# Two query projections moved in between the value tables by grid columns

## The chip, the cores and the metric

The kernel runs on one core of one Trainium2 chip, as one launch. Its time is the device time of that core in microseconds (us). Three runs of the kernel before gave 1713.64, 1715.28 and 1719.45 us; the median, 1715.28 us, is what the changed kernel is held against.

The engines are called as in the profile: PE is TensorE with its matmuls (PEld its weight loads), ACT is ScalarE, DVE is VectorE, POOL is GpSimd, SP is SyncE, which here only issues DMAs.

## The reference, cut to what matters

The model is a small audio tower of five steps on 4 batches of 750 tokens with 192 features. The change lies in the fourth, an attention with 12 heads of 64 features whose positions enter by two small tables, one by grid row and one by grid column (a grid of 27 columns):

```python
q = (x @ wq).reshape(B, N, H, HD).transpose(0, 2, 1, 3)
k = (x @ wk).reshape(B, N, H, HD).transpose(0, 2, 1, 3)
v = (x @ wv).reshape(B, N, H, HD).transpose(0, 2, 1, 3)
attn = jnp.einsum('bhid,bhjd->bhij', q, k) * scale
attn = attn + jnp.einsum('bhid,ijd->bhij', q, rel_pos_embed(N, rk_v, rk_h)) * scale
attn = jax.nn.softmax(attn, axis=-1)
out = jnp.einsum('bhij,bhjd->bhid', attn, v)
out = out + jnp.einsum('bhij,ijd->bhid', attn, rel_pos_embed(N, rv_v, rv_h))
out = out.transpose(0, 2, 1, 3).reshape(B, N, H * HD) @ wproj + bproj
```

## The kernel before, in words

The attention runs over 4 batches, each in two halves of 6 heads: eight half turns. A half turn has a long part, `words` (36 words of 125 keys each: scores, exponentials, values), and a passage from one half to the next. The first three batches are one hardware loop, the last batch is written out. There are seven passages that have a new half to prepare: four from half 0 to half 1 of one batch, three from half 1 to half 0 of the next batch. An eighth ends the attention and has no new half.

Every engine runs its own list of instructions in the order in which the code writes it, and the lists are tied by counting semaphores: `wait("name", k)` holds an engine until the k-th event of that name in this batch. Nothing is rearranged by a planner.

Keys and queries of a half are projected in six parts each (`keys_part`, `queries_part`; part n is pair n // 2 of heads, token half n % 2). A part is one `project` call: 5 matmuls of a full 128 x 128 weight tile over 376 columns (L2049) into bank n % 2 of the PSUM tile `a_M`. For keys, ACT copies the result to `khi` (L2391, two instructions) and DVE makes the rest `klo` (L2649, two). For queries, ACT copies to `pairs` (L2399, one). Before PE may write a bank again, its last reader must be done. Eight parts (half 0) or five parts (half 1) already run inside `words` between the last words (`fill`); what is left runs in the passage.

The passage of PE, in the order of its list before:

- the query parts that are left: parts 4 and 5 on the way from half 0 to 1, parts 1 to 5 on the way from half 1 to 0; then key parts 4 and 5;
- `value_tables` of the old half. One small product (L2104, L2107), then six sets by grid rows (`V_SETS`, L2117, weights of 96 rows x 64 columns), then six sets by grid columns (`H_SETS`, L2129, weights of 32 rows x 64 columns). ACT copies the first six out (L2432), DVE adds the last six to them (L2683). The fourth set by rows (m = 3) reuses the PSUM bank of the small product, and so waits for `rel_h_added` 1, which is DVE's copy of that product (L2677);
- `query_tables` of the new half (L2154, 128 rows x 64 columns, first by rows, `a_rqv`, then by columns, `a_rqh`), which wait for all six query parts in `pairs`; ACT and DVE copy them out in parallel (L2444, L2746);
- `boundary`: the values of the new half (L2193), the output projection of the old half (L2209) and the first row scores (L2167).

ACT's list in the passage: its output copies of the last word, the copies of the same parts, the six V copies, then `boundary`: six copies `work_rows` of the queries (L2405) and the table rows.

DVE's list in the passage from half 0 to half 1 reads: output of the last word (L2800, L2801), `keys_part` 4, `inverse`, `keys_part` 5, `value_tables`. `inverse` is a reciprocal (L2671) of softmax sums that come back by DMA: SP writes the sums to memory after the outputs (L1924, L1926), then fetches them as `dcol` (L1889). In the passage from half 1 to half 0 the order is: outputs, a bias add (L2641), `inverse`, `keys_part` 4 and 5, `value_tables`.

Of the kernel before, what the change touches and what calls it, by code (L numbers as in the profile page):

```python
# [1773 lines left out]
def window_attention(nc, keep, A, h, ident, W4, room, share, Y0, s_back, mv1, rstd1, w11, X1):  # L1774

    ctx = ExitStack()
    with ctx:
# [65 lines left out]
        def waiter(eng, i):  # L1843
            def wait(name, k):
                eng.wait_ge(sg[name], i * PER[name] + k)
            return wait
# [185 lines left out]
        def _(pe):  # L2032
# [17 lines left out]
                                            hn[:, m, lo:lo + HALF2], start=(x == 0), stop=(x == len(TERMS) - 1))  # L2050
                last.then_inc(sg[done], 1)

            def keys_part(i, half, n):

                wait = waiter(pe, i)
                if n == 0:
                    pe.wait_ge(s_wkv, 64 * i + 32 * half + 16)
                    wait("columns_ready", 3)
                elif n == 4 or n == 5:
                    wait("pairs_ready", half * 6 + n + 1)  # L2060
                elif n >= 2:
                    wait("khi_ready", half * 6 + n - 1)
                    wait("klo_ready", half * 6 + n - 1)
                project(wkv, n // 2, n % 2, 0, "k_product")

            def queries_part(i, half, n):

                wait = waiter(pe, i)
                if n == 0:
                    pe.wait_ge(s_wq, 32 * i + 16 * (half + 1))  # L2070
                if n < 2:
                    wait("khi_ready", half * 6 + n + 3)
                    wait("klo_ready", half * 6 + n + 3)
                else:
                    wait("pairs_ready", half * 6 + n - 1)
                project(wq, n // 2, n % 2, 1, "q_product")
# [17 lines left out]
                    elif x >= 35:  # L2094
                        queries_part(i + 1, 0, x - 35)

            def value_tables(i, half):

                wait = waiter(pe, i)
                wait("exp_ready", half * 36 + 36)  # L2100
                wait("out_dve", half * HG + HG)
                wait("out_act", half * HG + HG)
                for par in range(2):
                    nc.tensor.matmul(r_banks[0][64 * par:64 * par + 64, 0:NPR], rv[0:RH, 0, :],  # L2104
                                     work[0:RH, par::2, L - 1], start=True, stop=False)
                for par in range(2):
                    last = nc.tensor.matmul(r_banks[0][64 * par:64 * par + 64, 0:NPR], rv[RH:128, 0, :],  # L2107
                                            work[RH:128, par::2, CLS], start=False, stop=True)
                last.then_inc(sg["rel_product"], 1)
                for m, (gs, n) in enumerate(V_SETS):  # L2110
                    if m == 3:
                        wait("rel_h_added", half * (NHS + 1) + 1)
                    if m > 3:
                        wait("rel_v_copied", half * NV + m - 3)
                    for a, g in enumerate(gs):
                        for par in range(2):
                            last = nc.tensor.matmul(  # L2117
                                r_banks[(1 + m) % 4][64 * par:64 * par + 64, a * NPR * n:(a + 1) * NPR * n],
                                rv[0:RH, g + 1, :], group_tokens(work[0:RH, par::2, :], "v", g, n),
                                start=True, stop=True)  # L2120
                    last.then_inc(sg["rel_product"], 1)
                for m, (gs, n) in enumerate(H_SETS):
                    if m < 4:
                        wait("rel_v_copied", half * NV + NV + m - 3)
                    else:
                        wait("rel_h_added", half * (NHS + 1) + m - 2)
                    for a, g in enumerate(gs):
                        for par in range(2):
                            last = nc.tensor.matmul(  # L2129
                                r_banks[(1 + NV + m) % 4][64 * par:64 * par + 64, a * NPR * n:(a + 1) * NPR * n],  # L2130
                                rv[RH:128, g + 1, :], group_tokens(work[RH:128, par::2, :], "h", g, n),
                                start=True, stop=True)
                    last.then_inc(sg["rel_product"], 1)

            def query_tables(i, half):

# [183 lines left out]
            def turn(i, last_batch):  # L2320

                words(i, 0, last_batch)
                queries_part(i, 1, 4)
                queries_part(i, 1, 5)
                keys_part(i, 1, 4)
                keys_part(i, 1, 5)
                value_tables(i, 0)
                query_tables(i, 1)
                boundary((i, 0), (i, 1))
                words(i, 1, last_batch)  # L2330
                if last_batch:
                    value_tables(i, 1)
                    boundary((i, 1), None)
                else:
                    queries_part(i + 1, 0, 1)
                    queries_part(i + 1, 0, 2)
                    queries_part(i + 1, 0, 3)
                    queries_part(i + 1, 0, 4)
                    queries_part(i + 1, 0, 5)
                    keys_part(i + 1, 0, 4)  # L2340
                    keys_part(i + 1, 0, 5)
                    value_tables(i, 1)
                    query_tables(i + 1, 0)
                    boundary((i, 1), (i + 1, 0))

# [16 lines left out]
            with pe.Fori(0, B - 1) as i:  # L2362
                turn(i, False)
# [3 lines left out]
        def _(act):  # L2367
# [27 lines left out]
            def queries_part(i, half, n):  # L2395

                waiter(act, i)("q_product", half * 6 + n + 1)
                pr, a = n // 2, n % 2
                nc.scalar.activation(pairs[:, pr, a * HALF:(a + 1) * HALF], psM[:, a, a:a + HALF], ACT.Copy  # L2399
                                     ).then_inc(sg["pairs_ready"], 1)  # L2400

            def work_rows(i, half, x):

                waiter(act, i)("pairs_ready", half * 6 + 2 * (x // 2) + 2)
                nc.scalar.activation(work[0:64, x, 0:L], pairs[64 * (x % 2):64 * (x % 2) + 64, x // 2, :], ACT.Copy  # L2405
                                     ).then_inc(sg["work_ready"], 1)
# [30 lines left out]
            def boundary(old, new):  # L2437

                i, half = new
                wait = waiter(act, i)  # L2440
                if old is not None:
                    for x in range(HG):
                        work_rows(i, half, x)
                relative_rows(act, wait, half, 0, lambda o, x: nc.scalar.activation(o, x, ACT.Copy),  # L2444
                              "table_rows_act")
                wait("table_rows_act", (half + 1) * NTS)
                wait("table_rows_dve", (half + 1) * NTS)
                wait("work_ready", half * HG + HG)
                if old is not None:
                    waiter(act, old[0])("out_divided", old[1] * NPR + NPR)  # L2450
                else:

                    act.wait_ge(s_sum3, 3)
                for x in range(HG):
                    nc.scalar.activation(qhi[0:ONE, x, :], work[0:ONE, x, 0:L], ACT.Copy
                                         ).then_inc(sg["qhi_ready"], 1)
                    wait("v_product", half * CH + x + 1)
                    nc.scalar.activation(vhi[:, x, :, 0:64],
                                         psS[1][0:P, x % 2, 0:HG * HD].rearrange("p (h d) -> p h d", d=HD),
                                         ACT.Copy).then_inc(sg["vhi_ready"], 1)  # L2460
                    if old is None and x in (1, 2, 3):
                        for hh in (2 * x - 2, 2 * x - 1):
                            last = nc.scalar.activation(vhi[:, :, hh, 64:128], ohT, ACT.Copy)
                        if x == 3:
                            last.then_inc(s_og, 1)
                    if old is None and x == 4:
                        act.wait_ge(s_ln, 2)
                        nc.scalar.activation(rstd[:, CH:NT], rstd[:, CH:NT], ACT.Sqrt).then_inc(s_sd, 1)
# [58 lines left out]
            def turn(i, last_batch):  # L2527

                words(i, 0, last_batch)
                queries_part(i, 1, 4)  # L2530
                queries_part(i, 1, 5)
                keys_part(i, 1, 4)
                keys_part(i, 1, 5)
                value_tables(i, 0)
# [14 lines left out]
                else:  # L2549
                    queries_part(i + 1, 0, 1)  # L2550
                    queries_part(i + 1, 0, 2)
                    queries_part(i + 1, 0, 3)
                    queries_part(i + 1, 0, 4)
                    queries_part(i + 1, 0, 5)
                    keys_part(i + 1, 0, 4)
                    keys_part(i + 1, 0, 5)
                    value_tables(i, 1)
# [414 lines left out]
```

## Time and profile before

| | |
|---|---|
| median of 3 runs | 1715.28 us |
| the profiled execution | 1716.88 us, of which the span of the instructions is 1715.1 us |
| PE busy | 1539.9 us, 90% |
| DVE busy | 1172.9 us, 68% |
| ACT busy | 988.2 us, 58% |
| POOL busy | 374.2 us, 22% |
| mean granted clock of TensorE | 0.946 of full speed |

The attention fills the time from about 380 to 1490 us of the span. In it PE is busy nearly throughout. The granted clock is given as a share of full speed: 1.0 is 2.4 GHz, 0.5 is 1.2 GHz, and a value between them is the mean of a stretch that has both.

### The profile page before, as it was taken

The page shows a single profiled execution, that of the slowest core. Times are in us where ns is not written, and L with a number is a line of the kernel's source. Part 1 is how long each engine was busy: PE and PEld are TensorE (multiplying, and loading weights), DVE is VectorE, ACT ScalarE, POOL GpSimd, SP SyncE. Part 2 cuts the span into 40 slices and gives each one's busy share as a digit, 9 for nine tenths or more (in the row PEclk, how much of TensorE's full clock was granted, in tenths as well). Part 3 has the DMA queues.
Part 4 walks back from the last instruction along what each step waited for, and adds up shares of the span by engine and source line. Part 5 has one row for each costly group of instructions (what it writes and reads, how often), then busy time and mean ns, then how long its engine had stood idle before and what let it go on. Part 6 is the DMA issues. An engine that isn't in the chain of part 4 may idle for free. (4 is left out here: it accounts for less than half of the span.)

```text
span 1715.1 us, 32118 instructions
## 1 busy us (share of the span) xinstructions
PE 1539.9 (90%) x10815; PEld 1417.4 (83%) x10816; DVE 1172.9 (68%) x2224; ACT 988.2 (58%) x1777; POOL 374.2 (22%) x520
## 2 busy tenths in 40 slices
PE   5982999937999999999999999999999999848997
PEld 5862999936899898899998889988989988727996
DVE  4887555548775786786787677678677588585553
ACT  5541222225677578578677667767767857462231
POOL 5131566640001100110200110110100100013443
PEclk9995999977999999999999999999999999868998
DMA  9312111164101101100010110010010111091221
GB/s 267 70 55 77 48 57 57 57 142 121 44 11 38 45 11 39 46 11 19 25 49 11 31 45 20 30 44 20 29 45 11 39 49 37 21 295 49 61 58 28
DMA packets 61933, 94.81 MB, mean 55 GB/s; under 512 B 15644, under 2 KB 46511, under 8 KB 61422
## 3 DMA queue, kind: packets, MB, share of 16 engines
q1 hardware_dynamic: 52606, 72.92, 14.8%
q0 software_dynamic: 9200, 20.21, 4.1%
q8 instruction: 78, 1.28, 0.3%
q14 instruction: 49, 0.40, 0.1%
HBM read 72.58 MB, written 21.06 MB: 55 GB/s over the span
## 5 line engine op out<-in xcount | busy, mean ns | idle before, releaser
L2698 DVE TENSOR_REDUCE a_nmx<-a_M 125x1 f32<-125x752 f32 x256 | 240.8, 941 | 129.9 <-PE a_M L2167 129.2
L2517 ACT ACTIVATE a_Phi<-a_S 125x756 fp32r<-125x756 f32 x288 | 231.1, 803 | 156.9 <-PE a_O L2290 147.2
L2823 DVE TENSOR_TENSOR a_Plo<-a_PT,a_Phi 125x756 fp32r<-125x756 f32 x288 | 281.5, 977 | 52.5 <-ACT a_PT L2517 51.7
L2517 ACT ACTIVATE a_PT<-a_S 125x756 f32<-125x756 f32 x288 | 229.8, 798 | 0.0
L1970 POOL TENSOR_TENSOR a_qlo<-a_work,a_qhi 127x750 fp32r<-127x750 f32 x48 | 79.1, 1657 | 592.2 <-PE a_S L2271 507.9
L2271 PE MATMUL a_S<-a_qhi,a_khi 128*125 128x378 f32 x576 | 155.1, 350 | 13.6 <-issue 6.6
L2283 PE MATMUL a_O<-a_Phi,a_vhi 125*128 125x378 f32 x576 | 150.3, 342 | 1.3 <-ACT a_PT L2517 1.3
L2290 PE MATMUL a_O<-a_Plo,a_vhi 125*128 125x378 f32 x576 | 147.4, 337 | 1.0 <-DVE a_Plo L2823 0.9
L2271 PE MATMUL a_S<-a_qlo,a_khi 128*125 128x378 f32 x576 | 147.0, 336 | 0.0
L2271 PE MATMUL a_S<-a_qhi,a_klo 128*125 128x378 f32 x576 | 146.7, 336 | 0.0
L2286 PE MATMUL a_O<-a_Phi,a_vlo 125*64 125x378 f32 x576 | 146.4, 335 | 0.0
L2167 PE MATMUL a_M<-a_khi,a_qhi 127*125 127x376 f32 x512 | 132.2, 339 | 0.2 <-DVE a_nmx L2698 0.2
L1215 PE MATMUL m_psY<-m_w,m_hidT 128*128 x696 | 130.0, 330 | 2.6 <-DVE m_hidT L1572 2.6
L1215 PEld LDWEIGHTS m_psY<-m_w,m_hidT 128*128 128x128 f32 x696 | 114.4, 189 | 9.5 <-issue 9.5
L2271 PEld LDWEIGHTS a_S<-a_qhi,a_khi 128*125 128x125 f32 x576 | 98.3, 187 | 27.1 <-issue 13.6
L2290 PEld LDWEIGHTS a_O<-a_Plo,a_vhi 125*128 125x128 f32 x576 | 104.1, 189 | 14.5 <-DVE a_Plo L2823 4.3
L1299 ACT ACTIVATE m_xT<-m_psX 128x128 fp32r<-128x128 f32 x85 | 23.6, 278 | 156.4 <-PE m_psX L1139 156.4
L1979 POOL TENSOR_TENSOR a_outs<-a_outs,a_qhi 128x750 f32<-128x750 f32 x21 | 33.1, 1607 | 363.3 <-DVE a_outs L2683 363.3
L2283 PEld LDWEIGHTS a_O<-a_Phi,a_vhi 125*128 125x128 f32 x576 | 101.9, 190 | 11.1 <-issue 8.1
L1151 PE MATMUL m_psG<-m_w,m_xT 128*128 x540 | 110.4, 351 | 0.6 <-issue 0.4
L2271 PEld LDWEIGHTS a_S<-a_qhi,a_klo 128*125 128x125 f32 x576 | 103.9, 187 | 0.0
L2271 PEld LDWEIGHTS a_S<-a_qlo,a_khi 128*125 128x125 f32 x576 | 103.7, 187 | 0.0
(441 smaller groups left out, 3141.9 us busy)
## 6 DMA issues: line engine op xcount, KB each, us to landing
a_qhi<-a_rdens SPq DMA_DIRECT2D x48, 187.5 KB, 3.3
a_wkv<-a_w4k SPq DMA_DIRECT2D x8, 768.0 KB, 5.3
a_wq<-a_w4q SPq DMA_DIRECT2D x8, 768.0 KB, 6.7
a_wkv<-a_w4v SPq DMA_DIRECT2D x8, 768.0 KB, 5.8
m_w<-in_m_w SPq DMA_DIRECT2D x8, 576.0 KB, 9.2
m_X<-m_xn SPq DMA_DIRECT2D x8, 504.0 KB
m_w<-in_m_w SPq DMA_DIRECT2D x8, 384.0 KB, 7.3
m_w_ahead<-in_m_w SPq DMA_DIRECT2D x8, 384.0 KB, 8.0
```

The source lines that it names most:

```text
L1151: last = nc.tensor.matmul(psG[buf][:, g, 0:half], tokens, w1[0:rows_, bass.ds(e, 1), k, g * half:(g + 1) * half].rearrange("d o f -> d (o ...
L1215: last = nc.tensor.matmul(psY[:, 0:E], hidT[:, k * 128:(k + 1) * 128], w2[:, bass.ds(here, 1), k, :].rearrange("f o e -> f (o e)"), start= ...
L1970: pool.tensor_tensor(qlo[0:ONE, u % HG % QLO, :], work[0:ONE, u % HG, 0:L], qhi[0:ONE, u % HG, :].bitcast(F32), ALU.subtract).then_inc(sg[ ...
L1979: pool.tensor_tensor(outs[:, pr, 0:L], outs[:, pr, 0:L], rdb[:, pr, :], ALU.mult).then_inc(sg["out_divided"], 1)
L2167: last = nc.tensor.matmul(bank[0:P, a, 0:376], qhi[0:ONE, u % HG, c * P:(c + 1) * P], khi[0:ONE, u % HG, a * 374:a * 374 + 376], start=Tru ...
L2271: last = nc.tensor.matmul(psS[wd % 2][0:P, a, 0:HP], kk[:, u % HG, at], qq[:, PART[a]:PART[a] + HP], start=(x == 0), stop=(x == 2))
L2283: nc.tensor.matmul(psO[:, a, 0:HP], vhi[:, c, u % HG, :], Phi[:, wd % 2, at[a]], start=(c == 0), stop=False)
L2286: nc.tensor.matmul(psO[0:HD, a, 0:HP], vlo[:, c, u % HG, :], Phi[:, wd % 2, at[a]], start=False, stop=False)
L2290: last = nc.tensor.matmul(psO[:, a, 0:HP], vhi[:, c, u % HG, :], Plo[:, wd % 2, at[a]], start=False, stop=(c == CH - 1))
L2517: last = nc.scalar.activation(to[:, wd % 2, :].rearrange("p (a l) -> p a l", a=2), psS[wd % 2][0:P, :, 0:HP], ACT.Exp, scale=SCALE)
L2698: v.tensor_reduce(nmx[:, u % 2, c:c + 1], bank[0:P, :, 0:376], AX.XY, ALU.max, negate=True).then_inc(sg["max_ready"], 1)
L2823: v.tensor_tensor(Plo[:, wd % 2, :], PT[:, wd % 2, :], Phi[:, wd % 2, :].bitcast(F32), ALU.subtract).then_inc(sg["exp_rest"], 1)
```

## The change

On PE the two last query parts of every new half leave their place ahead of the key parts and go into `value_tables`, one behind the first set by grid columns (m = 0), one behind the third (m = 2). Key parts 4 and 5 move up. Since the order in which the banks of `a_M` are used is now keys 4, keys 5, queries 4, queries 5, the waits for a free bank are changed to match (`woven=True`): key parts 4 and 5 wait for query parts 2 and 3 to be copied, query parts 4 and 5 for key parts 4 and 5 to be split. ACT's copies of the two query parts move likewise, in between its `work_rows`. DVE, POOL and SP are not edited. The first half of the program, which has no old half, keeps its order, and so has the eighth passage.

```diff
-            def keys_part(i, half, n):
+            def keys_part(i, half, n, woven=False):
...
-                elif n == 4 or n == 5:
-                    wait("pairs_ready", half * 6 + n + 1)
+                elif n >= 4:
+                    wait("pairs_ready", half * 6 + (n - 1 if woven else n + 1))
...
-            def queries_part(i, half, n):
+            def queries_part(i, half, n, woven=False):
...
-                if n < 2:
-                    wait("khi_ready", half * 6 + n + 3)
-                    wait("klo_ready", half * 6 + n + 3)
+                if n < 2 or woven:
+                    wait("khi_ready", half * 6 + n + (1 if woven else 3))
+                    wait("klo_ready", half * 6 + n + (1 if woven else 3))
...
-            def value_tables(i, half):
+            def value_tables(i, half, new):
...
                     last.then_inc(sg["rel_product"], 1)
+                    if new is not None and m in (0, 2):
+                        queries_part(*new, 4 + m // 2, woven=True)
...
                 words(i, 0, last_batch)
-                queries_part(i, 1, 4)
-                queries_part(i, 1, 5)
-                keys_part(i, 1, 4)
-                keys_part(i, 1, 5)
-                value_tables(i, 0)
+                keys_part(i, 1, 4, woven=True)
+                keys_part(i, 1, 5, woven=True)
+                value_tables(i, 0, (i, 1))
...
                     queries_part(i + 1, 0, 3)
-                    queries_part(i + 1, 0, 4)
-                    queries_part(i + 1, 0, 5)
-                    keys_part(i + 1, 0, 4)
-                    keys_part(i + 1, 0, 5)
-                    value_tables(i, 1)
+                    keys_part(i + 1, 0, 4, woven=True)
+                    keys_part(i + 1, 0, 5, woven=True)
+                    value_tables(i, 1, (i + 1, 0))
...
                 if old is not None:
                     for x in range(HG):
+                        if x in (2, 4):
+                            queries_part(i, half, 3 + x // 2)
                         work_rows(i, half, x)
```

(The last piece is ACT's; two more pieces take `queries_part` 4 and 5 out of ACT's `turn`.)

PE's list in the passage from half 0 to half 1, from the last query part to the first query table. Before (`a_wq` are the query weights, `a_wkv` the key weights, `a_rv` the value tables; `x12` counts matmuls):

```order
646 L2049 MATMUL a_M<-a_hn,a_wq 128x376 x10
...
648 L2049 MATMUL a_M<-a_hn,a_wkv 128x376 x5
...
650 L2049 MATMUL a_M<-a_hn,a_wkv 128x376 x5
...
653 L2117 MATMUL a_O<-a_work,a_rv 64x81 x12
654 L2117 MATMUL a_S<-a_work,a_rv 64x81 x24
655 L1845 ISA
656 L2117 MATMUL a_O<-a_work,a_rv 64x81 x18
657 L2117 MATMUL a_S<-a_work,a_rv 64x60 x2
658 L2129 MATMUL a_S<-a_work,a_rv 64x84 x12
659 L2129 MATMUL a_O<-a_work,a_rv 64x84 x24
660 L2129 MATMUL a_S<-a_work,a_rv 64x84 x4
```

and now:

```order
646 L2049 MATMUL a_M<-a_hn,a_wkv 128x376 x10
...
649 L2117 MATMUL a_O<-a_work,a_rv 64x81 x12
650 L2117 MATMUL a_S<-a_work,a_rv 64x81 x24
651 L1845 ISA
652 L2117 MATMUL a_O<-a_work,a_rv 64x81 x18
653 L2117 MATMUL a_S<-a_work,a_rv 64x60 x2
654 L2129 MATMUL a_S<-a_work,a_rv 64x84 x12
...
656 L2049 MATMUL a_M<-a_hn,a_wq 128x376 x5
657 L2129 MATMUL a_O<-a_work,a_rv 64x84 x24
...
659 L2049 MATMUL a_M<-a_hn,a_wq 128x376 x5
660 L2129 MATMUL a_S<-a_work,a_rv 64x84 x4
```

The ten query matmuls have left the head of the passage and stand as two groups of five between the products by grid columns. The ISA row is the wait for `rel_h_added` 1 ahead of the fourth set by rows; it now stands ten matmuls nearer to the end of the words.

ACT's list from the last V copy on, before:

```order
342 L2432 ACTIVATE a_outs<-a_S 128x3x20
343 L2405 ACTIVATE a_work<-a_pairs 64x750 x6
344 L1845 ISA
345 L2444 ACTIVATE a_work<-a_S 29x3x162 x2
```

and now:

```order
341 L2430 ACTIVATE a_outs<-a_S 128x3x20
342 L2403 ACTIVATE a_work<-a_pairs 64x750 x2
343 L2397 ACTIVATE a_pairs<-a_M 128x375
344 L2403 ACTIVATE a_work<-a_pairs 64x750 x2
345 L2397 ACTIVATE a_pairs<-a_M 128x375
346 L2403 ACTIVATE a_work<-a_pairs 64x750 x2
```

The two copies of query parts stand behind the second and the fourth of the six row copies.

## Rows read from the trace of the kernel before

**Rows 1.** Seven passages, words' end to value products: us, PE busy, clock, DMA, GB/s.

```profile
530.97:552.90 21.93, 21.93 (x364) 0.84 0.18 56
666.94:690.21 23.27, 23.27 (x379) 0.93 0.21 53
804.67:827.17 22.50, 22.50 (x364) 0.85 0.19 55
940.36:963.89 23.53, 23.53 (x378) 0.93 0.20 53
1078.27:1097.70 19.43, 19.42 (x363) 1.00 0.21 64
1210.91:1234.43 23.52, 23.52 (x378) 0.93 0.18 53
1346.49:1367.45 20.96, 20.96 (x363) 0.92 0.21 59
```

**Rows 2.** PE in order of time, half 0 to 1, third batch: start, us.

```profile
1078.27 1.88 PE L2049 MATMUL a_M<-a_hn,a_wq 128*128 128x376 f32 x10
1080.08 1.99 PE L2049 MATMUL a_M<-a_hn,a_wkv 128*128 128x376 f32 x10
1082.01 0.28 PE L2104 MATMUL a_O<-a_work,a_rv 96*64 96x3 f32 x4
...
1083.32 1.85 PE L2117 MATMUL a_S<-a_work,a_rv 96*64 96x81 f32 x48
1085.00 1.43 PE L2117 MATMUL a_O<-a_work,a_rv 96*64 96x81 f32 x36
...
1086.48 1.11 PE L2129 MATMUL a_S<-a_work,a_rv 32*64 32x84 f32 x24
...
1090.58 1.91 PE L2154 MATMUL a_S<-a_pairs,a_rqv 128*64 128x81 f32 x48
```

**Rows 3.** PE in order of time, half 1 to 0, first to second batch.

```profile
666.94 4.65 PE L2049 MATMUL a_M<-a_hn,a_wq 128*128 128x376 f32 x25
...
673.24 0.28 PE L2104 MATMUL a_O<-a_work,a_rv 96*64 96x3 f32 x4
...
676.24 1.43 PE L2117 MATMUL a_O<-a_work,a_rv 96*64 96x81 f32 x36
```

**Rows 4.** Two stretches within the passage of the second batch, half 0 to 1.

```profile
814.00:816.00 2.00, 2.00 (x57) 0.91 0.90 229
816.00:818.00 2.00, 2.00 (x33) 0.50 0.72 263
```

**Rows 5.** DVE in order of time, same passage as rows 2.

```profile
1079.03 0.56 DVE L2801 COPY a_work<-a_O 32x378 f32<-32x378 f32 x1
...
1083.28 0.26 DVE L2671 RECIPROCAL a_dcol<-a_dcol 75x20 f32<-75x20 f32 x1
...
1084.71 0.16 DVE L2677 COPY a_outs<-a_O 128x3 f32<-128x3 f32 x1
```

**Rows 6.** SP's issue of `dcol` there; landing of all 24 such transfers.

```profile
1081.02 0.33 SPq L1889 DMA_DIRECT2D a_dcol<-a_dens  x1
```

```profile
DMA to landing us min/median/max: 1.5/1.7/3.1
```

**Rows 7.** DVE in order of time, same passage as rows 3.

```profile
675.76 0.16 DVE L2677 COPY a_outs<-a_O 128x3 f32<-128x3 f32 x1
```

**Rows 8.** ACT in order of time, same passage as rows 2.

```profile
1081.25 1.97 ACT L2391 ACTIVATE a_khi<-a_M 64x375 fp32r<-64x375 f32 x4 [0.59 <-PE a_M L2049]
...
1087.04 5.09 ACT L2405 ACTIVATE a_work<-a_pairs 64x750 f32<-64x750 f32 x6
```

**Rows 9.** PE in the eighth passage, which ends the attention.

```profile
1476.32 0.28 PE L2104 MATMUL a_O<-a_work,a_rv 96*64 96x3 f32 x4 [1.26 <-DVE a_work L2801]
...
1477.64 3.28 PE L2117 MATMUL a_S<-a_work,a_rv 96*64 96x81 f32 x48
```

**Rows 10.** Clock in the eighth passage: us, PE busy, clock, DMA, GB/s.

```profile
1478.00:1480.00 2.00, 2.00 (x34) 0.50 0.05 3
```

More of the change, by code:

```diff
@@ L2331, in turn @@
                 if last_batch:
-                    value_tables(i, 1)
+                    value_tables(i, 1, None)
                     boundary((i, 1), None)
@@ L2337, in turn @@
                     queries_part(i + 1, 0, 3)
-                    queries_part(i + 1, 0, 4)
-                    queries_part(i + 1, 0, 5)
-                    keys_part(i + 1, 0, 4)
-                    keys_part(i + 1, 0, 5)
-                    value_tables(i, 1)
+                    keys_part(i + 1, 0, 4, woven=True)
+                    keys_part(i + 1, 0, 5, woven=True)
+                    value_tables(i, 1, (i + 1, 0))
                     query_tables(i + 1, 0)
@@ L2529, in turn @@
                 words(i, 0, last_batch)
-                queries_part(i, 1, 4)
-                queries_part(i, 1, 5)
                 keys_part(i, 1, 4)
@@ L2552, in turn @@
                     queries_part(i + 1, 0, 3)
-                    queries_part(i + 1, 0, 4)
-                    queries_part(i + 1, 0, 5)
                     keys_part(i + 1, 0, 4)
```

## The prediction

> **What bounds the kernel now.** I read the page first: PE is busy 90% of the span, so in the attention time is won only by PE working faster or waiting less. Next the timeline of PE over the passages between halves, since the change lies only there. The reader is to see that PE has no idle time in them: busy time equals length in all seven [rows 1]. Yet the seven are not alike. They have the same work within each kind, and the four from half 0 to half 1 take 21.93, 22.50, 19.43 and 20.96 us. What goes with the length is the granted clock: 1.00, that is 2.4 GHz, in the shortest, and a mean of 0.84, 0.85 and 0.92 in the others [rows 1]. Read in short stretches it is not a clock a little lower: it is at 0.50 (1.2 GHz) for a while. In the second batch it falls between 814 and 816 us and is at 0.50 from 816 to 818 us, with PE busy all the time [rows 4]; PE was then at the products by grid columns, 32 rows of the array at a time, which in the undisturbed passage run without a break from 1086.48 to 1090.58 us [rows 2]. So something in this passage costs clock, though in one of seven it did not.
>
> What that costs is read from rows 1. From half 0 to 1, against the 19.43 us at full clock: 2.50, 3.07, 0 and 1.53 us, together 7.10. From half 1 to 0 there is no passage at full clock. I build one: its projections take 673.24 - 666.94 = 6.30 us [rows 3] where the other kind takes 1082.01 - 1078.27 = 3.74 [rows 2], so 19.43 + 2.56 = 21.99; the three lie over it by 1.28, 1.54 and 1.53 us, together 4.35. All falls in the seven passages cost 11.45 us, the most that a better clock can bring.
>
> **The work itself.** Ten query matmuls change place; nothing is added. They take 1080.08 - 1078.27 = 1.81 us [rows 2], 0.91 a part, at either place, so the moved work nets to nothing at full clock. It changes two things: what follows what, and who is late.
>
> **From half 1 to 0: who is late.** The value tables start 1.81 us earlier, and so does everything on ACT and DVE up to them, because both had been following PE there (in this passage `inverse` stands ahead of the key parts on DVE). DVE's copy of the small product would start at 675.76 - 1.81 = 673.95 and end at 674.11; PE wants the bank for its fourth set at 676.24 - 1.81 = 674.43 [rows 3, 7]. It fits with 0.3 us to spare. Cost: nothing.
>
> **From half 0 to 1: a new wait.** Here DVE's order is key part 4, `inverse`, key part 5, then the copy of the small product, and `inverse` doesn't follow PE but the output of the last word: SP issues the fetch of `dcol` at 1081.02 us whatever PE does, and it lands 1.7 us later, at 1082.72 [rows 6]. Before, the reciprocal came at 1083.28, after key part 4, and was not late [rows 5]. Now key part 4 is split early: `khi` takes half of 1.97 us [rows 8] from when ACT's output copies end at about 1079.6, where DVE's end too [rows 5], and DVE is ready for the reciprocal before 1082. So DVE sits until 1082.72. From the reciprocal's start to that of the copy are 1084.71 - 1083.28 = 1.43 us [rows 5]: copy from 1084.15 to 1084.31, and PE goes on some 0.1 us later, at 1084.41. (Estimate from rows 5 and 9: PE followed a DVE output that is as long after the last word by about that.) PE wants the fourth set at 1085.00 - (1082.01 - 1080.08) = 1083.07 [rows 2]. It waits 1.34 us. Behind this wait stand three sets by rows, all by columns, both query parts and the query tables, so nothing fills it. Four passages: 5.4 us. Both ends: with the quickest landing of 1.5 us the wait is 1.14 (4.6 us in all), with the slowest of 3.1 it is 2.74 (11.0 us) [rows 6]; I take the median, which is that of 24 like transfers. It cannot be below nothing: the value tables can't end sooner than PE's own work lets them.
>
> **ACT, and the query tables.** They wait for all six query parts. In the clock of rows 2, everything from the fourth set on lies 0.59 us earlier than before. ACT ends its V copies at 1087.04 - 0.59 = 1086.45, makes two row copies at 5.09 / 6 = 0.85 us [rows 8], copies query part 4, makes two more and is free for part 5 at about 1090.3; PE ends part 5 at about 1090.4. ACT has copied it by 1091.1, and PE ends the products by columns at 1090.58 - 0.59 + 1.81 = 1091.80. Margin 0.7 us, cost nothing, and ACT's last two row copies end by 1092.8, about when the first query table is ready. If this cover went, PE would wait what is missing, under 1 us a passage.
>
> **The clock.** Before, 4.10 us of 32-row products run in one piece. Now the pieces are 0.92, 1.84 and 1.34 us with 0.91 us of full-array matmuls between. Bounds: all falls go (-11.45 us), or none (0). The trace does not show a passage like the new one. What it does show is that the case is near an edge: the same products kept the clock once in seven [rows 1]. I take the share of full-array matmuls in the new stretch, 1.81 / 5.91 = 0.31, as the share of the cost that goes: -3.5 us. That is a guess between the ends; it lies nearer to none because each fall that stays costs as before, and because the new wait puts 1.34 us without any matmul just ahead of the weak products.
>
> **Sum.** +5.4 - 3.5 = +1.9 us. The profiled execution took 1716.88 us, 1.78 beyond its span, and would come to 1718.8; it stood 1.60 above the median of the runs, so against the median I forecast 1715.28 + 1.9 = 1717.2 us. A difference under 0.3% (5.1 us) can hardly be told from no change on this kernel.
>
> **Rivals.**
>
> A. *The clock holds in all seven.* For it: the one passage that kept it, and weak products now in pieces under 2 us. Against it: the falls are the rule, and the pieces still make up most of the stretch. -11.45 + 5.4 = -6.1: 1709.2 us. Chance 0.17.
>
> B. *The wait pulls the clock down.* The place is the wait before the fourth set by rows, from half 0 to 1. In the eighth passage PE stood idle for 1.26 us before the value tables; then the clock was at 0.50 [rows 10] and two sets by rows took 3.28 us against 1.85 [rows 2, 9]. If 1.34 us idle, followed within 1.5 us by the weak products, does the same, the fall starts early and the passage costs what the dearest one lost: 19.43 + 1.34 + 3.07 = 23.84 us, four times 95.4 against 84.8 now, +10.5; less 0.31 x 4.35 from the other three: +9.2, 1724.5 us. Each such passage is 1.8 us worse than in my sum, so it decides from two of four on. Against it: full work stands ahead of the wait, and in the eighth passage other gaps had come before. Chance 0.14.
>
> C. *The clock does not care for the weaving*, only the wait is felt: +5.4, 1720.7 us. What speaks for it: the clock fell with PE busy 22.50 of 22.50 us [rows 1], so busy time alone doesn't hold it, and I can't show from rows that array rows do. By the Trainium skill (TensorE: Matmul & The Clock Gate, section "HAM oscillation — how this bites in real kernels") the clock is lost through gaps in which the PE idles between bursts of matmuls. By that rule weaving full matmuls into a gapless row wins nothing and a new wait can only do harm. The trace does not agree with its first half, since the falls came without a gap. Chance 0.14.
>
> D. *The change doesn't make PE wait*, because the transfer is early or the bank is free sooner than I think: only the clock counts, -3.5, 1711.8 us. The rows leave little room for it: the fetch is issued at 1081.02 and even the quickest landing gives a wait. Chance 0.06.
>
> My forecast keeps 0.49.
>
> **How the numbers follow.** Faster than 1710.2: most of A and a little of the forecast and of D, 0.20. Slower than 1720.4: B, over half of C and a little of the forecast, whose landing can be slow, 0.26. Within: 0.54. The range reaches from A to nearly B: 1709 to 1723.5 us.
>
> **What would show it.** In the timeline of PE, from half 0 to 1, an idle time of 1.1 to 1.4 us before the fourth L2117 set, released by DVE's copy into `a_outs`, and DVE idle before its reciprocal until a DMA `a_dcol`; no such idle from half 1 to 0. The passages, cut as in rows 1: at a clock of 1.00 about 20.8 us (half 0 to 1) and 22.0 us (half 1 to 0). Mean clock over the seven between 0.91 and 1.00. Wrong would be: no wait at that set (D), a clock at 0.50 already in the sets by rows (B), or the same lengths of fall as before (C).

## The result, and the profile after

The changed kernel took 1753.07 us (median of 5 runs, 1744.31 to 1755.86), the kernel before in the same comparison 1717.71 us (5 runs, 1713.64 to 1723.38). The ratio is 1.021, with a 95% interval of 1.0185 to 1.0235: slower by about 36 us. The forecast was 1717.2 us and its range ended at 1723.5, so the direction was right, but the size was not: +1.9 us was forecast against 1715.28, about +35 came.

The profiled execution took 1744.31 us, with a span of 1742.5 us against 1715.1 before; PE is busy 1559.4 us against 1539.9, and the mean granted clock went from 0.946 to 0.926. The timeline of PE over the same seven passages as [rows 1] (window in us, length, PE busy, clock, DMA share, GB/s):

```profile
531.26:561.47 30.21, 27.84 (x363) 0.72 0.14 41
675.44:698.12 22.68, 22.67 (x378) 1.00 0.19 55
812.40:834.73 22.33, 20.12 (x364) 1.00 0.19 55
947.85:970.51 22.66, 22.65 (x378) 1.00 0.19 55
1084.89:1115.84 30.95, 28.64 (x363) 0.67 0.13 40
1229.11:1251.79 22.68, 22.67 (x378) 1.00 0.19 55
1363.67:1394.45 30.78, 27.84 (x363) 0.72 0.13 40
```

The seven come to 182.3 us against 155.1, and this difference of 27.2 us is nearly that of the spans, 27.4. So the loss of this execution lies in the passages, and within them it is all in one kind. The four from half 0 to half 1 (the uneven rows) take 114.27 us instead of 84.82, although PE has the same matmuls. Each now has idle time (length less busy: 2.37, 2.21, 2.31, 2.94 us), and three of four ran at a mean clock of about 0.7. The three from half 1 to half 0 take 68.02 us instead of 70.32 and all kept a clock of 1.00, which none of them had done before.

One passage of four kept its clock in this execution, which is the fastest of the five. Had it fared as the others, some 8.3 us more (30.65 less 22.33) would have brought 1752.6, about the median. That is an estimate, and not shown: the other four executions have no trace, and their mean granted clocks, 0.928 to 0.934, are not below the 0.926 of this one.

PE in the first passage, in order of time (start, us, line and operands, count, and in brackets the idle time before it and what ended it):

```profile
534.40 1.85 PE L2117 MATMUL a_S<-a_work,a_rv 96*64 96x81 f32 x48
538.62 2.34 PE L2117 MATMUL a_O<-a_work,a_rv 96*64 96x81 f32 x36 [2.37 <-DVE a_outs L2673]
...
541.10 1.94 PE L2129 MATMUL a_S<-a_work,a_rv 32*64 32x84 f32 x24
542.97 1.94 PE L2049 MATMUL a_M<-a_hn,a_wq 128*128 128x376 f32 x5
...
550.25 2.44 PE L2129 MATMUL a_S<-a_work,a_rv 32*64 32x84 f32 x32
552.90 3.43 PE L2156 MATMUL a_S<-a_pairs,a_rqv 128*64 128x81 f32 x48
```

The wait stands where the prediction put it, before the fourth set by rows, and DVE's copy of the small product (L2673, before L2677) releases it. But it is 2.37 us and not 1.34. And behind it everything takes 1.7 to 1.8 times as long: 24 products by columns 1.94 us, a query part 1.94 us. Compare the same rows at full clock, in the next passage:

```profile
683.04 1.43 PE L2117 MATMUL a_O<-a_work,a_rv 96*64 96x81 f32 x36
...
684.51 1.11 PE L2129 MATMUL a_S<-a_work,a_rv 32*64 32x84 f32 x24
685.55 1.13 PE L2049 MATMUL a_M<-a_hn,a_wq 128*128 128x376 f32 x5
686.61 2.00 PE L2129 MATMUL a_O<-a_work,a_rv 32*64 32x84 f32 x48
...
689.58 1.35 PE L2129 MATMUL a_S<-a_work,a_rv 32*64 32x84 f32 x32
691.00 1.90 PE L2156 MATMUL a_S<-a_pairs,a_rqv 128*64 128x81 f32 x48
```

Here a part takes 1.1 us, and the whole runs without a gap. In the clock of the first passage the loss is seen directly (window, length, PE busy, clock, DMA share, GB/s):

```profile
536.00:538.00 2.00, 0.25 (x8) 1.00 0.00 0
538.00:540.00 2.00, 1.38 (x26) 0.76 0.05 3
540.00:546.00 6.00, 6.00 (x65) 0.50 0.65 194
...
552.00:556.00 4.00, 4.00 (x62) 0.50 0.02 4
556.00:558.00 2.00, 2.00 (x33) 0.97 0.00 0
```

The clock is full up to the wait, falls within half a microsecond of its end and stays at 0.50 (1.2 GHz) through all that is left of the value tables and both query parts. It comes back only in the query tables, about 17 us later. PE is busy all that time. In the seven passages the clock was at 0.50 for 17.1, 0, 20.5 and 17.1 us from half 0 to 1, and never from half 1 to 0. Before, the falls were shorter (3.4 or 6.8 us) and began late, in the products by columns [rows 4] or just behind them.

The size of the wait has its own cause. DVE and SP, same passage (the columns are as for PE; the last line is the landing of all 24 such transfers):

```profile
536.96 0.27 DVE L2667 RECIPROCAL a_dcol<-a_dcol 75x20 f32<-75x20 f32 x1 [2.31 <-DMA a_dcol<-a_dens]
...
538.40 0.16 DVE L2673 COPY a_outs<-a_O 128x3 f32<-128x3 f32 x1
```

```profile
534.01 0.33 SPq L1889 DMA_DIRECT2D a_dcol<-a_dens  x1
```

```profile
DMA to landing us min/median/max: 1.5/1.7/3.5
```

From the issue at 534.01 to the reciprocal at 536.96 are 2.95 us, where the prediction had 1.7. From the reciprocal to the copy are 1.44 us, where it had 1.43. In the four passages the transfer lands after 2.92, 2.75, 2.86 and 3.48 us, and each wait is the landing less 0.55 us. At the same place of the kernel before it took 1.64, 1.72, 1.49 and 1.51 us.

What lengthened it is in the DMA view of the stretch in which it lands (the stretch in 40 slices, busy tenths; then queues with packets, MB and share):

```profile
DMA  0090024543000000000000000010100000000000
...
DMA packets 166, 0.02 MB, mean 12 GB/s; under 512 B 165, under 2 KB 165, under 8 KB 165
...
q8 instruction: 1, 0.02, 3.8%
```

The kernel before, the same transfer (533.7 to 535.4 us):

```profile
DMA  0000000000000000000000355410012000000000
...
DMA packets 165, 0.01 MB, mean 4 GB/s; under 512 B 165, under 2 KB 165, under 8 KB 165
```

`dcol` consists of 165 small packets. After the change there is one packet more, of 16 KB, on the queue that carries program code. It occupies one DMA engine for 3.8% of 16 x 1.8 us, about 1.1 us, and just then most of the small packets go through in a burst, while the last 11 come over a microsecond late (the ones to the right). There are 78 such code packets in both kernels. In the four passages from half 0 to 1 one starts 3.4 to 3.8 us from the passage's start, within the transfer (at 534.8 us in the first), where before it came at 4.8 to 5.5 us, after it (at 536.1). Ten matmuls that stood ahead of its place in PE's list now stand behind it. In each of the four, 11 of the 165 packets come late; before, in none.

This was to be seen in the trace of the kernel before. Of its 24 landings seven took 2.5 to 3.1 us, and in each of these a code packet started 0.4 to 1.2 us after the issue. The other 17 took 1.5 to 2.1 us, and none of them had a code packet there.

### The profile page after: what moved, and what is told of

Its sections match the earlier page's. It is cut to its first block and busy times, and to the rows that moved or that the text cites. A ratio compares the mean times of both kernels' runs of the same rounds, so it can differ in the third digit from the quotient of the medians.

```text
span 1742.5 us, 32132 instructions
## 1 busy us (share of the span) xinstructions
PE 1559.4 (89%) x10815; PEld 1428.9 (82%) x10816; DVE 1173.1 (67%) x2224; ACT 987.8 (57%) x1777; POOL 374.1 (21%) x520
## 3 DMA queue, kind: packets, MB, share of 16 engines
q8 instruction: 78, 1.28, 0.3%
## 5 line engine op out<-in xcount | busy, mean ns | idle before, releaser
L2273 PE MATMUL a_S<-a_qhi,a_khi 128*125 128x378 f32 x576 | 155.1, 350 | 13.5 <-issue 7.0
```

What stands on the lines that cost most here:

```text
L2273: last = nc.tensor.matmul(psS[wd % 2][0:P, a, 0:HP], kk[:, u % HG, at], qq[:, PART[a]:PART[a] + HP], start=(x == 0), stop=(x == 2))
```

## The experiments

Ten kernels ran. The intervals are of the ratio to the kernel before. Theory 1: the new wait pulls the clock down (rival B, at a larger size). Theory 2: the new order does it by itself.

### The wait taken away

```diff
                 v.tensor_copy(outs[:, :, 0], r_banks[0][:, 0:NPR]).then_inc(sg["rel_h_added"], 1)
+                if inverse_here:
+                    inverse(i, half, NPR - 1)
...
                 keys_part(i, 1, 4)
-                inverse(i, 0, NPR - 1)
                 keys_part(i, 1, 5)
-                value_tables(i, 0)
+                value_tables(i, 0, True)
```

> The changed kernel, but DVE makes key part 5 and the copy of the small product ahead of its reciprocal in the passage from half 0 to 1, so that the DMA can't hold PE. Theory 1 (the wait takes the clock, the weaving is sound): no idle time at the fourth set by rows; all seven passages at full clock, about 20.1 us each from half 0 to 1 (19.43 and some 0.6 for the changes between kinds of product) and 22.7 from half 1 to 0; against the kernel before 4 x 20.1 + 3 x 22.7 - 155.1 = -6.6 us, some 1711. Theory 2 (the new order itself loses the clock from half 0 to 1, with the wait or without): passages of 28 to 31 us there as in the changed kernel, 1745 us or more.

Measured: 1712.93 us against 1719.07, ratio 0.9959 (0.9942 to 0.9975). One passage of each kind:

```profile
534.73:554.66 19.93, 19.92 (x363) 1.00 0.22 62
668.65:691.33 22.68, 22.67 (x378) 1.00 0.19 55
```

No passage has a wait and all seven kept a clock of 1.00. They sum to 147.7 us. `dcol` still landed late (2.6 to 3.2 us), and it cost nothing, since nobody needs it. That moving one reciprocal on DVE turns +2.1% into -0.4% shows that the loss is the wait and what follows from it. Theory 2 falls. So does another thought, that DMA traffic takes the clock (it is dense where the clock fell, [rows 4]): it is as dense here, at a share of 0.19 to 0.22, and the clock held.

The same edit on the kernel before:

> The kernel before with DVE's order alone mended (key part 5 and the copy of the small product ahead of the reciprocal, from half 0 to 1). PE did not wait there before, so if the gain of no_wait comes from the weaving, this is no different from the kernel before: within 0.2%, falls in the products by columns in most passages. If DVE's order were itself the gain, some 6 us faster.

Measured: ratio 1.0003 (0.999 to 1.0016), no difference. So the edit has no worth of its own, and the 0.4% is the woven order's. In this trace four of seven passages lost clock, against six in the trace of the kernel before: how many fall varies between executions. It also has a passage from half 1 to 0 at full clock, 22.02 us; the prediction had built 21.99.

### A wait put into the kernel before

Copies of the same bank into a tile of their own, ahead of DVE's copy of the small product in half 0, so that PE waits with nothing woven. Eight, 15, 24 and 40 of them:

```diff
+                if half == 0:
+                    for k in range(24):
+                        v.tensor_copy(pad[:, k], r_banks[0][:, 0:NPR])
                 v.tensor_copy(outs[:, :, 0], r_banks[0][:, 0:NPR]).then_inc(sg["rel_h_added"], 1)
```

> The kernel before, with 8 small copies to a tile of their own on DVE ahead of the copy that PE's fourth set by rows waits for, from half 0 to 1: a wait of about 1.3 us, the size that the prediction gave the new wait. Theory 1a (any wait there will do): the clock falls in the sets by rows in most of the four passages, +12 us or more. Theory 1b (its length matters): the wait alone is felt, 4 x 1.3 = 5 us, and the clock falls as before, in the products by columns; 1720 to 1725. Theory 2: as 1b.

> The kernel before, with 15 such copies: a wait of about 2.4 us, as long as measured in the changed kernel. Theory 1 (the wait takes the clock): a clock of 0.50 from the sets by rows on in at least three of the four passages, +15 us or more over the kernel before. Theory 2 (the new order does it): only the wait is felt, 4 x 2.4 = 9.6 us, about 1727.

Both missed the size that they were made for, since such a copy in a row takes 67 ns and not the 160 ns of a single one. The waits (releaser, sum in us, times, longest), eight copies and then 15:

```profile
PE a_O L2118 <- DVE a_outs L2681: 1.1, 4, 0.3
```

```profile
PE a_O L2118 <- DVE a_outs L2681: 3.0, 4, 0.8
```

Ratios 1.003 (1.0014 to 1.0046) and 1.0027 (1.001 to 1.0044). With a mean of 0.28 and of 0.75 us the clock did not fall early; it fell only in the products by columns or just behind them, as before. The ratio with eight copies is over what 1.1 us of waiting explain (0.06%); the number and length of the late falls varies, and I leave it there. A second pair had the sizes meant:

> The kernel before with 24 small copies of 67 ns each on DVE ahead of the copy that PE's fourth set by rows waits for. The runs with 8 and 15 made waits of 0.28 and 0.75 us, not the 1.3 and 2.4 us meant; this one makes about 1.3 us, the size in the prediction. Theory 1a (any wait from there on will do): the clock at 0.50 from the sets by rows on in most of the four passages, +12 us or more. Theory 1b (a short one doesn't): 4 x 1.3 = 5 us over the kernel before, falls only in the products by columns as before. Theory 2 (not the wait but the new order loses the clock): as 1b.

> The same with 40 copies: a wait of about 2.4 us, as long as measured in the changed kernel. Theory 1: the clock at 0.50 from the sets by rows on in at least three of the four passages, each at 26 us or more, +15 us or more over the kernel before. Theory 2: only the wait is felt, 4 x 2.4 = 9.6 us, some 1729.

With 24 copies, a wait of 1.35 us: ratio 1.0082 (1.0054 to 1.0111). With 40, 2.43 us: 1.0171 (1.0132 to 1.0211). The first and the last passage with 24, then the same two with 40:

```profile
530.45:556.19 25.74, 24.39 (x363) 0.80 0.17 48
...
1360.96:1385.12 24.16, 22.80 (x363) 0.86 0.18 51
```

```profile
531.46:558.28 26.82, 24.39 (x363) 0.81 0.16 46
...
1366.22:1394.63 28.41, 25.98 (x364) 0.76 0.16 43
```

From half 0 to 1 the passages take 24.2 to 25.8 us with 1.35 us and 26.7 to 28.4 with 2.43, the clock at 0.50 for 6.8 to 10.2 and for 10.2 to 13.7 us. All eight fell, seven of them earlier than before: 1.7 to 2.4 us from the start of the fourth set with 24 copies (the last one 4.0, as late as before) and 0.05 to 2.6 us with 40, against 4.2 to 5.1 us in the kernel before. So a wait at this place is enough to pull the clock down early, without any weaving, and costs 3.4 to 6.6 us beyond its own length (against 19.43), where the falls of the kernel before cost 1.8 in the mean. That the longer wait also costs more clock is not shown: three of four passages have 10.2 us at 0.50 with either, and the means are 4.6 and 5.3 us.

### The weaving undone, the wait kept

```diff
-                    if new is not None and m in (0, 2):
-                        queries_part(*new, 4 + m // 2, woven=True)
+                    if new is not None and m == NHS - 1:
+                        queries_part(*new, 4, woven=True)
+                        queries_part(*new, 5, woven=True)
```

> The changed kernel with query parts 4 and 5 behind all value tables instead of between them: the same wait of 2.2 to 2.9 us, no weaving. Theory 1 says that the clock falls as in the changed kernel. If the woven parts do not help a fallen clock up, and are themselves slowed, the time at 0.50 is not longer here: 1740 to 1753. If they do help it up, it is over 1755. From half 1 to 0 the falls in the products by columns come back, about 23.5 us a passage instead of 22.7.

Measured: 1759.19 us, ratio 1.023 (1.0206 to 1.0254), with waits of 2.08 to 2.82 us. The first and the last of the four passages:

```profile
534.21:563.16 28.95, 25.43 (x364) 0.76 0.15 43
...
1384.74:1415.37 30.63, 26.73 (x364) 0.72 0.14 40
```

The four take 28.9 to 30.6 us. By the time alone, over 1755, this would be the case in which the woven parts help a fallen clock up. The trace doesn't say so: the clock falls in all four and is at 0.50 for 13.7 to 17.1 us, not longer than the 17.1 to 20.5 of the three falls with the weaving. The excess has other causes. There is a flaw in the design: with both parts last, PE also waits 1.08 us for ACT's copy of part 5, seven times. And from half 1 to 0, with no wait at the sets by rows, the clock fell in all three again (24.61, 27.46, 27.44 us). To see the weaving alone, the same with the wait taken away too:

> The run not_woven, with DVE's order mended as in no_wait: query parts behind the value tables, no wait at the fourth set. It tells what the weaving alone does. If the woven parts hold the clock, here it falls in the products by columns in most passages, as before (6 of 7), and with the 1.1 us for which PE waits for ACT's copy of part 5 it costs some 20 us over no_wait: about 1732. If the clock in no_wait was held by the missing wait or by luck, it holds here too: about 7 x 1.1 = 8 us over no_wait, 1721.

Measured: ratio 1.0082 (1.0054 to 1.011). Two of its passages:

```profile
530.84:555.25 24.41, 23.33 (x364) 0.79 0.18 51
...
1358.24:1379.55 21.31, 19.51 (x363) 1.00 0.20 58
```

Four of seven fell, with the products by columns in one piece, where woven without a wait none did. The first of them (window, length, PE busy, clock, DMA share, GB/s):

```profile
537.00:540.00 3.00, 3.00 (x85) 1.00 0.06 7
540.00:542.00 2.00, 2.00 (x38) 0.68 0.67 164
...
```

PE is busy for all 5 us, and the clock goes at the end of the products by columns, ahead of the wait for ACT (that came at 545 us). The other three falls also began 3.0 to 7.3 us before PE went on after that wait, so it did not cause them. This is the fall of the kernel before, without a gap.

### The code packet moved away from the transfer

Four small matmuls are added at each change of head in the words of half 0, 20 in a half; what they write is overwritten. They shift the work at which code is fetched.

```diff
+                    if half == 0 and c == 0 and u > u0:
+                        for _ in range(4):
+                            nc.tensor.matmul(psO[0:64, 1, 500:503], rv[0:RH, 0, :], rv[0:RH, 1, 0:3],
+                                             start=True, stop=True)
```

> The changed kernel with 20 small matmuls more in the words of half 0 (96 rows, 3 columns, results overwritten), which set every 16 KB block of PE's program some 80 instructions further along the work. If the block fetch at the value tables delays the landing of dcol, it now comes about 1.5 us sooner in the passage, the landing is back at 1.5 to 1.7 us, the wait is 1.0 to 1.3 us and the clock falls in fewer passages or later. If something else in the new order slows the landing, it stays at 2.7 to 3.5 us and the wait at 2.2 to 2.9 us.

One execution, 1740.24 us, the added matmuls' own time included. The code packet now comes at 532.2 us, and the transfer at 534.6 to 536.5 us looks as it did before the change:

```profile
DMA  0000000000000000000354510000000000000000
...
a_dcol<-a_dens SPq DMA_DIRECT2D x1, 5.9 KB, 1.5
```

In none of the four passages does a code packet start between issue and landing. `dcol` lands after 1.50, 1.74, 1.65 and 1.54 us and PE waits 0.94, 1.19, 1.14 and 0.99 us. DVE's reciprocal there, and the four passages:

```profile
536.10 0.27 DVE L2671 RECIPROCAL a_dcol<-a_dcol 75x20 f32<-75x20 f32 x1 [0.88 <-DMA a_dcol<-a_dens]
```

```profile
531.83:552.92 21.09, 20.13 (x364) 1.00 0.21 59
806.80:834.25 27.45, 26.26 (x364) 0.75 0.16 45
1087.40:1108.67 21.27, 20.11 (x363) 1.00 0.20 58
1359.44:1386.74 27.30, 26.31 (x364) 0.75 0.15 45
```

So the collision is what made the landing long. And even with the landing that the prediction had used, the clock falls in two of four, which costs 6 us each: the four passages take 97.1 us against 84.8 before, with waits of only 4.3 us. A passage either keeps its clock and takes 21.1 us, or takes 27.4. Of four waits between 0.94 and 1.19 us, it was not the two longest that fell (0.99 did, 1.14 did not): near one microsecond this is open.

### Both parts behind the second set by columns

As the first experiment, with one interruption instead of two:

```diff
-                    if new is not None and m in (0, 2):
-                        queries_part(*new, 4 + m // 2, woven=True)
+                    if new is not None and m == 1:
+                        queries_part(*new, 4, woven=True)
+                        queries_part(*new, 5, woven=True)
```

> The run no_wait with both query parts together behind the second set by columns (m = 1) instead of one behind the first and one behind the third. Each change between kinds of product cost some 0.15 us at full clock, and there are two fewer: about 0.3 us less in each of seven passages, 2 us less than no_wait if the clock holds (about 0.5% under the kernel before). If the clock needs the even spacing, it falls in some passages, 1.5 us each, and the run is no better than no_wait or worse.

Measured: 1706.56 us (8 runs) against 1713.36 (20 runs), ratio 0.9961 (0.9948 to 0.9974). All seven passages kept the clock:

```profile
528.62:548.19 19.57, 19.56 (x363) 1.00 0.22 63
662.17:684.50 22.33, 22.32 (x378) 1.00 0.19 56
```

They sum to 145.2 us, 2.5 less than in the first experiment, which the ratios can't tell apart. Both versions beat the two kernels.

## Why the prediction was wrong, step by step

**The step that failed is the clock term, -3.5 us.** The prediction let the new wait cost nothing but its own length and took a part of the old falls away. In the seven passages of the profiled execution the clock cost +13.3 us instead: +17.6 from half 0 to 1, where the wait pulled it down, and -4.35 from half 1 to 0. The waits were 9.8 us and not 5.4, and the weaving itself cost 4.0 and not nothing. Together that is the 27.2 us. The steps one by one:

**Where, who and what releases it: right.** The wait stands at the fourth set by rows, from half 0 to 1 only, released by DVE's copy, because DVE sits in front of its reciprocal until `dcol` lands. From half 1 to 0 there is none, and at full clock none before the query tables, as forecast.

**"It waits 1.34 us": the mis-sized term.** It measured 2.46 us in the mean, 9.8 us in all instead of 5.4. The working behind it holds: with a landing of 1.5 to 1.74 us the wait was 0.94 to 1.19, within 0.2 us of landing less 0.36. The input failed. I took the median of 24 landings for a place whose landing had a reason to change. The slowest, 3.1 us, was in the profile [rows 6] and was treated as bad luck; it and the six others over 2.1 us belonged to transfers that meet a code packet, and the change moves instructions, and so the packets, against the transfers. My upper bound, 11.0 us for the four, did hold this term.

The Trainium skill (Runtime: NRT & Kernel Launch, section "Instruction fetch mechanics") has code fetched in 16 KiB blocks through the sequencer's own DMA queue, at a cost that it calls mostly hidden. The trace agrees on the size (78 packets, 1.28 MB). The page speaks of what crossing a block costs the engine whose code it is, and in these passages PE indeed has no other wait. But for the kernel the cost was not hidden: one packet put 1.0 to 2.0 us on another queue's transfer, and this one was waited for.

**Rival B was the case, and both its chance and its price were too low.** It had 0.14, and 23.84 us for a passage. The three that fell took 30.2 to 31.0 us: 19.93, the wait, and 7.9 to 8.7 us for the clock, where I had put 3.07. That price was "what the dearest one lost" [rows 1], from a fall that begins in the products by columns and ends soon after in the query tables. A fall that begins at the wait lasts until the same query tables, so it runs over three sets by rows, all sets by columns and both query parts as well. I priced the depth of a fall by rows and took its length from a place where it starts later. The length could have been estimated from rows: by the prediction's own times the work from the fourth set to the first query table is 1091.80 - 1084.41 = 7.39 us at full clock, and at half clock it takes up to as much again. The first passage shows where the 7.9 us went: that stretch took 552.90 - 538.62 = 14.28 us, against 691.00 - 683.04 = 7.96 in the next passage, which is 6.3 more, and the query tables, in which the clock came back, some 1.5 more. The eighth passage [rows 9, 10], which had shown a fall beside a gap, was evidence that I discounted because other gaps had come before it.

**The account for the four passages from half 0 to 1**, +29.45 us: waits +9.8, weaving 4 x (19.93 - 19.43) = +2.0, and clock 24.7 against 7.1, +17.6.

**"the share of the cost that goes", 0.31: too low where there is no wait, meaningless where there is one.** Without the wait all of it goes, 7 of 7 passages in each of two kernels. That the pieces between full-array work hold the clock is shown by the pair with both parts behind the products (4 of 7 fell) and with one part behind the first and third set (0 of 7), although the first of these also has a wait for ACT, which came behind all four falls.

**"the moved work nets to nothing at full clock": small, but wrong.** The four changes between kinds of product cost 0.5 us from half 0 to 1 (19.93 against 19.43) and 0.66 from half 1 to 0 (22.68 against 22.02), some 4 us over the seven. With two changes instead of four, 0.14 and 0.31 are left. That is why the three passages from half 1 to 0 gained 2.3 us and not the 4.35 that their falls had cost.

**Rival A** (1709.2) had the clock right for a kernel without the wait, not for this one. **Rival C** and the Trainium skill's rule on gaps: a gap did cost clock here, so the half that speaks against the change was right. Its other half, that weaving wins nothing, is refuted by the first experiment. **Rival D** falls: the wait was there four times of four.

Why a passage now and then keeps its clock after a wait of 2.2 us, or loses it at 0.99, stays open.

## What to carry to other kernels

A wait on a busy PE in front of work that fills little of the array, as here, is priced by two terms: its own length, and the work until the clock comes back, which here took 1.7 to 1.8 times as long. Read from your traces in which work the clock comes back (here the query tables), how far that is from the wait, and count it at that rate, with a microsecond or two of the query tables themselves. Before moving work, ask who will wait for a transfer that nobody waited for till now, take the slow landings of the trace as places and not as scatter, and let the instructions that don't need the transfer go first: here one reciprocal moved behind a key part and a 0.16 us copy was worth 2.5%.

## What the runs showed of the hardware that was not expected

- The clock fell with PE busy without a break, in 32-row products or just behind them (in 6 of 7 passages, and in 4 of 7 with DVE's order changed), and in none of 14 once full-array matmuls stood between them and no wait came ahead.
- Ahead of the fourth set by rows, means of 0.28 and 0.75 us of waiting started no early fall; 0.94 to 1.19 us did in 2 of 4 (woven order); 1.35 us in 3 of 4 and 2.43 us in 4 of 4 (order of before); 2.2 to 2.9 us in the changed kernel in 3 of 4. This is of this place only.
- After an early fall, 32-row products and even single full-array parts of 5 matmuls did not bring the clock back; in the changed kernel it came back in the query tables each time. Where ten full-array matmuls stood in one piece behind the products, it once came back at their end (837.7 us, in the run that undoes the weaving and keeps the wait).
- A code packet of 16 KB, about 1.1 us on one DMA engine, made a transfer of 165 small packets land after 2.5 to 3.5 us instead of 1.5 to 2.1.
- Copies of 128 x 3 elements in a row take 67 ns each on DVE, where a single one takes 160 ns.
